# Max-search matmuls ahead of the short job and the value product, and the first reduction ahead of the short copy, in every slot of a decoder layer

## The reference

```
x = layernorm(x + self_attention(x))            # iterated, 3 rounds
x = layernorm(x + cross_attention(x, memory))   # 16 heads, 512 queries, 1601 keys
x = layernorm(x + ffn(x))                       # base product + one of 8 adapters

# cross attention, per batch and head:
scores = (q @ k.T) / 4;  p = softmax(scores);  out = p @ v;  return out @ Wo.T
# ffn: the adapter with the smallest reconstruction loss is chosen per batch
```

## Time and profile before

| | |
|---|---|
| median of 3 runs | 1773.57 us (1770.79 to 1775.18) |
| the profiled execution, its own time | 1775.18 us |
| its span | 1773.4 us |
| TensorE busy | 1635.7 us (92%) |
| VectorE busy | 1235.8 us (70%) |
| ScalarE busy | 1059.2 us (60%) |
| batches 1 to 6 | from 360.1 to 1524.7 us |

### The profile page before, as it was taken

How to read it: one execution, slowest core, us unless ns; L and a number is a source line. 1 busy time by engine, 2 the same in 40 slices (tenths; PEclk the granted TensorE clock), 3 DMA queues, 4 the chain that set the end, 5 groups by cost and what they waited for, 6 DMA issues and landing times.

```text
span 1773.4 us, 25671 instructions
## 1 busy us (share of the span) xinstructions
PE 1635.7 (92%) x9786; PEld 611.3 (34%) x9786; DVE 1235.8 (70%) x1811; ACT 1059.2 (60%) x1987; POOL 163.5 (9%) x150
## 2 busy tenths in 40 slices
PE   5664988999999999999999999999999999999875
PEld 4341322333233333343343323333334324332232
DVE  4555766787778867787778777786778777777322
ACT  1110666676666766666666666666666666666740
POOL 5410100010001000110001000110001000000000
PEclk9775999999999999999999999999999999999987
DMA  4343416060705234161707061342507050600000
GB/s 127 84 102 87 83 49 113 6 122 24 131 25 93 64 78 78 38 106 27 128 16 132 26 119 38 68 90 64 92 1 135 22 82 25 107 2 1 4 24 16
DMA packets 99936, 116.59 MB, mean 66 GB/s; under 512 B 20811, under 2 KB 85196, under 8 KB 99813
## 3 DMA queue, kind: packets, MB, share of 16 engines
q1 hardware_dynamic: 97076, 113.89, 32.1%
q10 hardware_dynamic: 2736, 1.06, 0.2%
HBM read 80.12 MB, written 34.78 MB: 65 GB/s over the span
## 4 chain that ended last, share of the span: by engine, by line
PE 78%; issue 4%; ACT 4%; DVE 3%; DMA 1%; ACTq 0%; POOLq 0%; POOL 0%; SPq 0%; DVEq 0%
PE banks L1052 21%; PE values L1069 21%; PE banks L1029 11%; PE work L937 4%; PE work L951 4%; ACT xprobs L1165 4%; PE work L907 4%; PE work L958 3%; PE work L964 3%; PE work L892 3%; PE work L967 1%; PE work L943 1%; DVE xneg_max_pieces L1353 1%; PE work L976 1%; DMA ctxT_b<-in_ctxT 1%
## 5 line engine op out<-in xcount | busy, mean ns | idle before, releaser
L1165 ACT ACTIVATE xprobs<-banks 128x512 f32<-128x512 f32 x1664 | 902.6, 594 | 464.0 <-PE banks L1052 449.3
L1353 DVE TENSOR_REDUCE xneg_max_pieces<-banks 128x2 f32<-128x1024 f32 x768 | 909.2, 1220 | 273.2 <-PE banks L1029 271.0
L1052 PE MATMUL banks<-xq_stacks,xk_stacks 99*128 99x512 bf16 (+1 forms) x1664 | 523.1, 385 | 34.5 <-ACT xprobs L1165 23.0
L1069 PE MATMUL values<-xprobs,xv_rows 128*17 128x512 f32 x3328 | 437.9, 598 | 1.0 <-ACT xprobs L1165 1.0
L1052 PEld LDWEIGHTS banks<-xq_stacks,xk_stacks 99*128 99x128 bf16 (+1 forms) x1664 | 127.9, 97 | 427.4 <-ACT xprobs L1165 281.4
L1029 PE MATMUL banks<-xk_stacks,xq_stacks 49*128 49x512 bf16 (+1 forms) x2048 | 252.5, 339 | 14.5 <-DVE xneg_max_pieces L1353 9.9
L1029 PEld LDWEIGHTS banks<-xk_stacks,xq_stacks 49*128 49x128 bf16 x2048 | 56.7, 94 | 285.7 <-DVE xneg_max_pieces L1353 164.5
L1418 POOL TENSOR_TENSOR xk_parts<-xk_rest,xk_parts 128x401 bf16<-128x401 f32 (+1 forms) x64 | 58.9, 921 | 700.9 <-ACT xk_parts L1130 700.9
L1069 PEld LDWEIGHTS values<-xprobs,xv_rows 128*17 128x17 f32 x3328 | 55.1, 95 | 119.9 <-issue 118.5
L1413 POOL TENSOR_TENSOR xrstd<-xrstd,mhalf 128x4 f32<-128x4 f32 x23 | 23.2, 1010 | 665.2 <-DVE xrstd L1225 665.2
L1116 ACT ACTIVATE xk_parts<-work 128x401 bf16<-128x401 f32 (+1 forms) x64 | 32.4, 507 | 57.0 <-PE work L937 57.0
(11 more groups left out here) (250 smaller groups left out, 1092.5 us busy)
## 6 DMA issues: line engine op xcount, KB each, us to landing
xk_stacks<-key_parts_dram SPq DMA_DIRECT2D x192, 200.1 KB, 11.9
key_parts_dram<-xk_parts SPq DMA_DIRECT2D x144, 100.0 KB, 1.7
xq_stacks<-parts_dram SPq DMA_DIRECT2D x192, 64.0 KB, 8.0
ctxT_a<-in_ctxT SPq DMA_DIRECT2D x4, 1601.0 KB, 7.4
ctxT_b<-in_ctxT SPq DMA_DIRECT2D x4, 1601.0 KB, 8.6
parts_dram<-xq_parts SPq DMA_DIRECT2D x48, 128.0 KB, 1.9
key_parts_dram<-xk_parts SPq DMA_DIRECT2D x48, 100.2 KB, 7.9
xa<-in_x SPq DMA_DIRECT2D x8, 512.0 KB, 14.3
```

The lines of the kernel that those rows point to most:

```text
L1052: pe.matmul(scores[n % SRING], kst[0:ROWS[par], k, h2, par, t * P:(t + 1) * P], qst[0:ROWS[par], k, h2, par, :], start=True, stop=True).th ...
L1069: last = pe.matmul(av[32 * j:32 * j + HD + 1, :], vals[:, k, t, gr * GH + j, :], probs[:, sl % 2, j, :], start=t == 0, stop=t == XKT - 1)
L1165: nc.scalar.activation(probs[:, sl % 2, j, :], scores[n % SRING], ACT.Exp).then_inc(exped, 1)
L1353: nc.vector.tensor_reduce(nmp[:, of % 2, j2, :, q, piece], pairs[n % MRING][:, :, :], AX.X, ALU.max, negate=True).then_inc(mxr, 1)
```

## The change

On TensorE the two pair units P0, P1 now come right after S1; the short job follows, and V comes last before S2. On VectorE R0 now comes before the short job's copy out of `W`. Nothing is added or taken away, and ScalarE's list, the DMA queues and all waits stay as they are.

```
@@ pe_slot
             pe_scores(m, t, 0)
             pe_scores(m, t, 1)
+            for one in pairs_at(m, t):
+                pe_next_pair(*one)
+            if short:
+                pe_job(MAIN, short)
             if sl:
                 pe_values(sl - 1)
-            if short:
-                pe_job(MAIN, short)
-            for one in pairs_at(m, t):
-                pe_next_pair(*one)
             pe_scores(m, t, 2)
             pe_scores(m, t, 3)
@@ dve_slot
             if parts:
                 dve_max_parts(MAIN, m + 1, 0)
+            if todo:
+                dve_next_pair(*todo[0])
             if in_between(sl):
                 dve_job(MAIN, in_between(sl))
-            if todo:
-                dve_next_pair(*todo[0])
             if parts:
```

## The result

The changed kernel takes 1796.83 us (median of 4 runs, 1794.81 to 1801.33), the kernel before, run beside it, 1774.38 (4 runs, 1770.79 to 1776.01). The sign was right and so were many of the places, but the size was about twice too large.

A forecast was written before the change was run, and what follows sets the result against it. TensorE was taken as the bound. Waits of 4.9 + 0.9 + 0.7 + 0.9 = 7.4 us a batch, 49 in all with the shorter end batches, gave a median of 1823; own range 1805 to 1842, 8 in 10 1796 to 1850.

The forecast's parts named there:

- Part 1: TensorE's array-form edges: P to V costs 0.13 us like V to P, so the order alone changes nothing; bounds −35 and +27.
- Part 2: TensorE reaches the short job 0.45 us too early and waits for copies out of `W`; 4.9 us a batch.
- rival *faster: Earlier reductions free `W` sooner where its copy stood directly behind R1 (slots 10, 12, 49); 7 us, 1766; chance 0.06.
- Part 3: VectorE's short copy behind R0 holds `W` longer: 0.47 us in slot 36, 0.2 each in 10 and 49; 0.9 a batch.
- Part 4: Late R0 on VectorE stops P1 (slots 7, 38): 0.7 us a batch; ScalarE's later value copy delays exponentials: 0.9.
- VectorE falls behind: Rival: late R0 makes P1 stop TensorE in 20 or so slots a batch, 48 us more in all, 1871; chance 0.10.
- P to V costs nothing: Rival: TensorE's edge from P to V is free, the rest of the forecast stands; 1788 us; chance 0.10.

The follow-up runs named there:

- e5: Kernel before, with the changed order on both engines in slots 4, 8 and 41 only; 1787.56 us in one run, against 1772.34 for before.
- e1: TensorE in the changed order, VectorE's list as before (short copy ahead of R0); 1797.75 us, ratio 1.0158 to the kernel before.
- e4: Changed kernel, but with the old order on both engines in the first slot of each group; 1798.82 us, ratio 1.0164 to the kernel before.

## Why the prediction was half right

**Part 1, the bare order: right.** P to V 0.54, V to S2 0.99, where V to P was 0.99 and P to S2 0.53. The edges before and after sum to the same.

**Part 2, the short job too early: right behind key and query projections, wrong behind value tiles and output products.** Slots 1, 11 and 35 lost 0.36 where 0.37 was said, with the release that was named. (Part 2 lists slots 4, 8, 12, 14 and 41 as behind a value tile; 8 stands behind an output product, 12 behind a key projection and 14 behind a query projection.) What failed is the sentence "No copy gets earlier, since VectorE waits there for the end job, which ends when it did". It is true behind key and query projections, whose copy waits for ScalarE's copy of the same bank. Part 2 itself says otherwise for slots 10 and 49, where the copy "was late behind reductions that now end sooner", and did not carry this over to the others. In slots 4, 8, 10, 41 and 49, and on the way to slot 7, the copy is of a value tile or an output product, and before the change it had long had its data: it stood behind R1 of its own engine. R1 moved 0.98 us up with P, and the copy with it, 0.6 to 0.9 us. Slots 4, 8 and 41 were to cost 1.3 and gave 0.1; slots 10 and 49 were to cost 0.7 and gave 0.4; slot 7 was to cost 0.4 and cost nothing. Together 2.9 of the 3.6 us a batch by which the forecast was too high (0.3 of them, in slots 10 and 49, for another reason: V beside the transposes, below). e5 shows it: the same edit in slots 4, 8 and 41 without an earlier R1 costs 0.45 to 0.54 in each. In the row I used for it, 764.84, no idle time stands in brackets, and R1 ended at 764.93: the copy stood behind R1. That it could move shows only beside the other end, that of the value tile 0.63 us earlier; in slot 36 the bracket is missing too, and the copy stayed.

The same reading would have told more of the rival *faster*: it named copies directly behind R1 and priced slots 10 and 49 at 0.4 each, which is what e1 gives for TensorE's half (0.45); its third slot, 12, lost time. I had it denied for slot 4 by rows that show just that.

Three slots fell short for reasons of their own. In slot 12 the transposes start 2.16 us behind S0 both times, since they wait for the norm's application, and V in place of P behind them costs the 0.44 (S2 at 3.26 before, 3.70 after). But 0.10 comes back at the end job: before, its first weight load started with its first matmul, released by ScalarE's copy, and after the change it is done ahead. In slots 23 and 36 V runs beside the `max` transposes: 0.32 and not 0.44. Slot 2 lost 0.46, more than the 0.37, because its P holds the unit of the left-over keys and takes 0.44 and not 0.53, so TensorE arrives sooner and waits longer.

**Part 3, `W` held behind R0: right in the mechanism,** 0.62 us of slot 36 by e1 against 0.47, and 0.23 against 0.2 each in slots 10 and 49. The 0.15 more in slot 36 is 0.05 of a later start and 0.1 which the key projection takes longer after a wait: 1.45 us from its start to the next S0 where it is 1.35 when TensorE comes to it without one (897.66 to 899.11 in the changed kernel, 896.51 to 897.86 in e1). In slots 10 and 49 the later start is 0.13 and this 0.1 makes the rest, so the fit with 0.2 is in part luck. The smaller loss in slot 36 from part 2 made up for it.

**Part 4, VectorE and ScalarE: right for slot 38 (0.26 against 0.35), wrong for slot 7** (the failed sentence again), and 0.20 instead of 0.31 for ScalarE, because an exponential starts 0.49 us after the start of a copy whose record is 0.60 long. I took the record's end; the distance between starts would have been right, as on TensorE. In slot 14 only 0.10 of it shows, the rest falls into the short job's wait.

**The ends of the kernel.** The first batch was to cost 3.4 and gave 0.6, the last to cost 1.5 and gave 0.65. In the first, 2.1 us of the cost came (slots 11, 14, 23, 26, 36 and 40), and slots 10 and 49 gained 0.45 each, against 0.22 later on. Another 1.7 were gained in slots 0, 1 and 25, which are in no term of the prediction: in slot 25 a wait for the transfer of the maxima was 1.0 us shorter, for which I have no cause. In the last batch slots 10 and 41 gained 0.45 and 0.48, which no term had.

**The rivals.** That VectorE falls behind in some 20 slots did not happen: P1 is stopped by R1 in slot 38 alone. That P to V costs nothing is excluded by the rows of slot 31, so that the time came out nearer to its 1788 than to my 1823 is a coincidence.

**Left open.** Whether ScalarE's 0.20 in three slots can be saved was not shown by e4.

## What to carry to other kernels

Before an edit that moves work of one engine, read for every copy that frees a shared buffer what it started behind: the producer, or the instruction ahead of it on its own engine. Read both ends, that of the instruction ahead and that of everything the copy waits for (the code lists it; the view names one): the later end holds the copy, and it can move forward by no more than the distance between the two. In slot 4 that was 0.63 us, and a cost of 0.44 became a gain; in slot 36, which also shows no idle time in front of its copy, it was nothing. Then ask slot by slot how much work covers the copy in the new order, look at the slot in front as well, since an early slot behind a late one paid 0.15 to 0.59 us, and keep the order only where slots gain: four slots, on TensorE alone, gave −0.44%, where all 52 on both engines gave +1.3%.

## What was not expected of the hardware

V begins 0.01 us after the `max` transposes (L979, 32 columns, ahead of V's four strips of 17) in slots 10, 23, 36 and 49, while P began 0.16 after them. In slot 1, behind the 128-column transposes, V does not begin so early: 0.58 us after the first of four, as P did before (0.59). It is worth 0.12 us in slot 23 (0.32 lost where 0.44 was worked out) and about 0.15 in slots 10 and 49. The runs don't tell which property of the two programs makes it.

After a wait, the fp32 key projection takes 0.1 us longer than without one (1.45 against 1.35), so a wait of TensorE before such a job costs more than its own length. The trace shows where it goes. In e1 the first weight load of the projection starts at 896.29, beside the scores and 0.22 ahead of the first matmul; in the changed kernel it starts only when the wait ends, at 897.66 together with the first matmul, whose record is 0.60 long and not 0.50. The query projection in slot 49 shows the same: 0.96 us to the next S0 after a wait, 0.86 without.

On ScalarE, an activation of 128x512 that is recorded with 0.60 us lets the next one start 0.49 after it.
